# Self-attention of a three-stage block: scores a step ahead, token rows, V with zero blocks, and the softmax's sum before the next maximum

## The chip, the cores and the metric

The program runs on one core of a Trainium2 chip. Its time is the device time of one execution in microseconds (us). Its engines run side by side and meet at semaphores: TensorE (PE, matmul; PEld is its weight load), VectorE (DVE), ScalarE (ACT), GpSimd (POOL), and SyncE (SP), which here only issues DMAs. Each takes its own instructions in order: what stands behind a waiting instruction waits too.

## The reference, cut to what matters

```
x = x + cross_attention(layernorm(x), ctx)      # stage 1
x = x + self_attention(layernorm(x))            # stage 2, the one that is changed
x = x + gated_ffn(layernorm(x))                 # stage 3

# stage 2, x of shape (32, 64, 256), 16 heads of 16:
qkv = x @ W_w.T + W_b
attn = q k^T / 16;  attn[future] = -inf;  attn += rpb[position difference]
o = softmax(attn) @ v                            # one 64x64 matrix per batch element and head
y = x + o @ proj_w.T + proj_b;  out = layernorm(y) * ln_g + ln_b
```

Its 2048 rows (32 batch elements of 64 tokens) are 16 tiles of 128: two batch elements a tile.

## The kernel before, in words

Stage 2 is `self_attention` (lines 838 to 1351); stages 1 and 3 stand before and behind it, each closed by a barrier of all engines, and are not touched.

**Preparation.** DVE normalises the tiles (`normal`). Work of four tiles (a group r of 0 to 3) is cut into units, listed in `SETUP` (before the loop) and `BESIDE` (units inside step s): TN transposes rows, QK makes a 128x512 block of queries or keys (PE; ACT evicts it twice, as float16 QK_HI and as float32; POOL makes QK_LO, their difference), VV makes V rows (DVE evicts them), WT transposes part of stage 3's gate weight, and XT transposes the result for stage 3. For every group SP then issues 36 DMAs that stack the three float16 products (hi·hi, hi·lo, lo·hi) in 96 partitions: 12 into SQS (queries, L940), 24 into KZ (keys, L948), whose other half-heads are zeros that POOL has written (L1153, L1165). PE waits for the 36 at the first tile of a group. SP's first wait is for QK_LO (L935).

**The loop** runs s from 0 to 18, a pipeline over tiles:
- PE: scores of tile s (L1012, 32 matmuls of 64 columns), `PT`x`V` of tile s-2 (L1025, 32 matmuls with 16 columns of V), projection of s-3 (L1037, 4 matmuls), the step's units, and last the eight transposes of tile s-1's probabilities (L1050), which wait for POOL's scaling of s-1.
- DVE: add the bias to the scores (L1291, into T), row maximum (L1295), both of tile s; then residual and statistics of s-3 (L1299, L1301), units, and last sum and reciprocal of s-1 (L1312, L1314).
- POOL: subtract the maximum, tile s (L1175); scale by the reciprocal, tile s-1 (L1180).
- ACT: copy PT and OT of tile s-2 (L1112, L1115), lay V of s-1 into VS with zeros around it (L1122), exponential of tile s (L1125), and units behind it.

Scores stand with (head parity, query) in the partitions, so bias and V have to be repeated or laid out for each of the two batch elements w. In steps 13 to 16 DVE also has the end of the layer norm: `scale_rows` (aggregates and twelve small dependent operations) and `add_rows` (three operations a tile).

The order within each engine is the order of the statements. The steps are unrolled by Python, without a planner.

Of the kernel before, what the change touches and what calls it, by code (L numbers as in the profile page):

```python
# [43 lines left out]
C_ID, C_HM, C_DM, C_IQ, C_HQ, C_B1 = 0, 128, 130, 138, 202, 204  # L44
C_ALL = C_B1 + 1


def constants():
    c = np.zeros((P, C_ALL), np.float32)
    p = np.arange(P)  # L50
    c[:, C_ID:C_ID + P] = np.eye(P)
    for a in range(2):
        c[:, C_HM + a] = (p % 32) // DH == a
        c[:, C_HQ + a] = np.where(p < ROW_M, c[:, C_HM + a], 1.0)
    for j in range(PAIRS):
# [755 lines left out]
def turned(xr, c):  # L811
# [8 lines left out]
]  # L820
BESIDE = {
# [7 lines left out]
NARROW = 2  # L829
NORMS = [(0, 10), (10, 14), (14, 16)]  # L830
# [7 lines left out]
def self_attention(nc, sb, ctx, dram):  # L838
# [4 lines left out]
    def psum(name, shape):  # L843
# [16 lines left out]
    V = alloc("V2", [P, TILES, D], F32)  # L860
    VS = alloc("VS", [P, 2, 2, D], F32)
# [6 lines left out]
    OT = alloc("OT2", [P, 2, 4, P], F32)  # L868
# [3 lines left out]
    WN = PT[:, :, :, :].rearrange("p u j r -> p (u j r)")[:, 0:WCOLS]  # L872
# [9 lines left out]
             "vs bias_ok xb init zeroed s_ps t_a t_max t_sub t_exp t_sum t_norm p_ps pt pv ot y_ps y_sb y_stat "  # L882
# [3 lines left out]
    N_SMALL = 5  # L886
    PARTS = 36

# [17 lines left out]
    def emptied(eng, x):  # L906

        done = {"TN": "xlo", "QK": "qk_32", "VV": "v_sb", "WT": "wg_lo", "XT": "xt_sb"}[x[0]]
        eng.wait_ge(sm[done], number[x] + 1)

    def qk_rows(i):
        return i
# [12 lines left out]
    def _(sp):  # L925
        sp.dma_start(WRAW[:, :, :], dram["w_t"].rearrange("(k p) n -> p k n", p=P)).then_inc(sm["in_w2"], 16)
        sp.dma_start(BQK[:, :], dram["bqk"]).then_inc(sm["in_small"], 16)
        for tile, name in ((BV, "bv2"), (LG, "ln_g"), (LB, "ln_b")):
            sp.dma_start(tile[:, :], dram[name].rearrange("(a d) -> a d", a=1).broadcast_to([P, D])).then_inc(sm["in_small"], 16)
        sp.dma_start(BIAS[:, :, :], dram["bias"]).then_inc(sm["in_small"], 16)  # L930
        sp.dma_start(WN.rearrange("p (f d) -> p f d", f=FT), dram["w_gate"].rearrange("(f p) d -> p f d", p=P)).then_inc(sm["in_wg"], 16)
        sp.dma_start(WP[:, :, :], dram["wp"]).then_inc(sm["in_wp"], 16)
        for r in range(TILES // 4):
            u = r % 2
            sp.wait_ge(sm["qk_lo"], 4 * r + 2)  # L935
            if r >= 2:
                sp.wait_ge(sm["s_ps"], 4 * (r - 1))
            for c in range(4):
                for q, part in enumerate((QK_HI, QK_HI, QK_LO)):
                    sp.dma_start(SQS[32 * q:32 * q + 32, u, c::4, :], part[32 * c:32 * c + 32, u, 0:2, :]).then_inc(stacked[r], 16)  # L940
            sp.wait_ge(sm["qk_lo"], 4 * r + 4)
            if r < 2:
                sp.wait_ge(sm["zeroed"], r + 1)
            for c in range(4):
                for q, part in enumerate((QK_HI, QK_LO, QK_HI)):
                    for a in range(2):
                        lo = 32 * q + DH * a
                        sp.dma_start(KZ[lo:lo + DH, u, c::4, a, :], part[32 * c + DH * a:32 * c + DH * a + DH, u, 2:4, :])\  # L948
                            .then_inc(stacked[r], 16)
        for r in range(TILES // 4):  # L950
            sp.wait_ge(stacked[r], 16 * PARTS)

    @block.tensor
    def _(pe):

        def setup(x):
# [11 lines left out]
            elif kind == "QK":  # L968
                m = qk_rows(i)
# [5 lines left out]
                for e, (w, h, k) in enumerate([(w, h, k) for w, h in ((WHI, 0), (WHI, 1), (WLO, 0)) for k in range(KT)]):  # L975
                    last = pe.matmul(bank, w[:, k, m * P:(m + 1) * P], XR[:, r, h, k, :], start=(e == 0), stop=(e == 5))
                last.then_inc(sm["qk_ps"], 1)
            elif kind == "VV":
                pe.wait_ge(sm["xlo"], 2 * r + 2)
                for s in range(2):  # L980
                    lo = (2 * i + s) * P
                    for e, (h, w, k) in enumerate([(h, w, k) for k in range(KT) for h, w in ((0, WHI), (0, WLO), (1, WHI))]):
                        last = pe.matmul(bank[:, s * D:(s + 1) * D], XR[:, r, h, k, lo:lo + P], w[:, k, 2 * D:3 * D],
                                         start=(e == 0), stop=(e == 5), skip_group_check=True)
# [14 lines left out]

        for x in SETUP:  # L1000
            setup(x)
        for s in range(STEPS):
            if live(s):
                r, lo = s // 4, s % 4 * P
                if s % 4 == 0:
                    pe.wait_ge(stacked[r], 16 * PARTS)
                need(pe, sm["t_a"], s)
                for j in range(PAIRS):
                    for w in range(2):
                        cols = slice(lo + w * SQ, lo + (w + 1) * SQ)  # L1010
                        for a in range(2):
                            last = pe.matmul(S_PS[SQ * a:SQ * (a + 1), (2 * j + w) * SQ:(2 * j + w + 1) * SQ], SQS[0:96, r % 2, j, cols],  # L1012
                                             KZ[0:96, r % 2, j, a, cols], start=True, stop=True, skip_group_check=True)
                last.then_inc(sm["s_ps"], 1)
            if live(s - 2):
                t = s - 2
                if t == 0:
                    pe.wait_ge(sm["init"], 3)
                pe.wait_ge(sm["pt"], t + 1)
                pe.wait_ge(sm["vs"], 2 * t + 2)  # L1020
                need(pe, sm["ot"], t)
                for w in range(2):
                    for h in range(H):
                        row = 32 * (h % 4)
                        last = pe.matmul(O_PS[row:row + DH, (h // 4) * P + w * SQ:(h // 4) * P + (w + 1) * SQ],  # L1025
                                         VS[:, t % 2, w, h * DH:(h + 1) * DH],
                                         PT[:, t % 2, h // 2, (h % 2) * SQ:(h % 2 + 1) * SQ],
                                         start=True, stop=True, skip_group_check=True)
                last.then_inc(sm["pv"], 1)
            if live(s - 3):  # L1030
                t = s - 3
                if t == 0:
                    pe.wait_ge(sm["in_wp"], 16)
                pe.wait_ge(sm["ot"], t + 1)
                need(pe, sm["y_sb"], t)
                for g in range(4):
                    last = pe.matmul(Y_PS[:, 0:D], OT[:, t % 2, g, :], WP[:, g, :], start=(g == 0), stop=(g == 3))  # L1037
                last.then_inc(sm["y_ps"], 1)
            for x in BESIDE.get(s, []):
                setup(x)  # L1040
            if live(s - 1):
# [7 lines left out]
                for j in range(PAIRS):  # L1049
                    last = pe.transpose(T_PS[:, j * P:(j + 1) * P], T[:, t % 3, j, :, :].rearrange("p w k -> p (w k)"),  # L1050
# [6 lines left out]
    def _(act):  # L1057

        def setup(x):
# [3 lines left out]
            if kind == "TN":  # L1063
# [35 lines left out]

        act.wait_ge(sm["ln2"], LN_ROOT)  # L1100
        nc.scalar.activation(SD[:, :], VE[:, :], ACT.Sqrt).then_inc(sm["root2"], 1)
        for x in SETUP:
            setup(x)
        act.wait_ge(sm["init"], 3)
        for s in range(STEPS):
            if live(s - 2):
                t = s - 2
                if t == 0:
                    act.wait_ge(sm["wg_lo"], 4)
# [5 lines left out]
                nc.scalar.activation(OT[:, t % 2, :, :], O_PS[:, :].rearrange("p (g r) -> p g r", g=4), ACT.Copy).then_inc(sm["ot"], 1)  # L1115
            if live(s - 1):
                t = s - 1
                need(act, sm["pv"], t - 1)
                act.wait_ge(sm["v_sb"], t // 2 + 1)
                for w in range(2):  # L1120
                    rows = slice(64 * w, 64 * w + 64)
                    nc.scalar.activation(VS[rows, t % 2, w, :], V[rows, t, :], ACT.Copy).then_inc(sm["vs"], 1)  # L1122
# [8 lines left out]
            for x in BESIDE.get(s, []):  # L1131
                setup(x)
# [9 lines left out]
    def _(pool):  # L1142

        def setup(x):

            kind, r, i = x
            if kind == "QK":
                n, m = number[x] + 1, qk_rows(i)
                pool.wait_ge(sm["qk_32"], n)
                pool.tensor_tensor(QK_LO[:, r % 2, m, :], QK32[:, (n - 1) % 3, :], QK_HI[:, r % 2, m, :], ALU.subtract)\  # L1150
                    .then_inc(sm["qk_lo"], 1)

        pool.memset(KZ[:, 0].rearrange("p j a c -> p (j a c)").bitcast(F32), 0.0).then_inc(sm["zeroed"], 1)  # L1153
# [579 lines left out]
```

## Time and profile before

| | us |
|---|---|
| median of 3 runs (1729.69, 1731.11, 2875.7) | 1731.11 |
| the profiled execution: device time | 1730.49 |
| its span, first to last instruction | 1728.7 |
| stage 2 in it: 1246.69 to 1541.46 | 294.8 |
| of that, before the first scores (1299.07) | 52.4 |

Busy over the whole span: PE 84%, DVE 63%, ACT 52%, POOL 49%. In stage 2 alone the sums are PE 155.4, DVE 151.3, POOL 104.9 and ACT 96.1 us of 294.8, so no engine is full there; what counts is what each waits for. The 2875.7 is one run far off the other two.

### The profile page before, as it was taken

To read this page: it belongs to the slowest core of one execution; us is meant where nothing else is said; L and a number is where in the kernel's file an instruction comes from. 1 tells how busy PE (TensorE), PEld (TensorE's weight loads), DVE (VectorE), ACT (ScalarE), POOL (GpSimd) and SP (SyncE) were. 2 spreads that over 40 slices of the span, in tenths; PEclk is the share of its full clock that TensorE was granted. 3 is DMA by queue.
4 is the path that set the end of the run, shared out by engine and by line. 5 is a ranking of instruction groups with operands and counts; after the bars stand their busy time and mean duration, and the time that the engine had idled before them with its cause. 6 is when DMAs were issued, how large, how long until landed. Compare 5 with 4: busy or idle time off the path is not lost. (4 is left out here: it accounts for less than half of the span.)

```text
span 1728.7 us, 55875 instructions
## 1 busy us (share of the span) xinstructions
PE 1450.7 (84%) x24601; PEld 1018.8 (59%) x24601; DVE 1081.6 (63%) x1736; ACT 900.0 (52%) x1196; POOL 839.4 (49%) x555
## 2 busy tenths in 40 slices
PE   3789999999999999999999999999655655457607
PEld 2357777677776777766777767777424444333206
DVE  7656666666666666666666666666353444586985
ACT  1446555566556665566665556656433322143752
POOL 5567655666655666556665566653053443202000
PEclk9899999999999999999999999999876876678958
DMA  5544544334444344443454534543122110010001
GB/s 171 134 118 103 126 115 136 105 98 123 120 112 133 98 117 123 114 134 98 108 129 108 143 99 101 128 115 69 31 70 52 26 38 1 1 37 0 1 0 49
DMA packets 90688, 154.94 MB, mean 90 GB/s; under 512 B 17280, under 2 KB 55816, under 8 KB 90448
## 3 DMA queue, kind: packets, MB, share of 16 engines
q1 hardware_dynamic: 89088, 150.40, 33.4%
q8 instruction: 195, 3.19, 0.8%
q10 hardware_dynamic: 1360, 0.98, 0.2%
q14 instruction: 45, 0.37, 0.1%
HBM read 60.95 MB, written 2.20 MB: 37 GB/s over the span
## 5 line engine op out<-in xcount | busy, mean ns | idle before, releaser
L639 DVE TENSOR_REDUCE MXP<-W_PS 128x1 f32<-128x512 f32 x768 | 499.2, 688 | 283.4 <-PE W_PS L451 283.4
L535 ACT ACTIVATE PR<-S_PS 128x1024 f32<-128x1024 f32 (+1 forms) x416 | 424.9, 1023 | 258.6 <-PE S_PS L399 250.8
L345 POOL TENSOR_TENSOR K_HI<-K,MCOL 128x512 f16<-128x512 f32 (+1 forms) x224 | 219.0, 978 | 425.3 <-ACT K L543 424.0
L347 POOL TENSOR_TENSOR K_LO<-K,K_HI 128x512 f16<-128x512 f32 (+1 forms) x224 | 291.8, 1302 | 17.6
L451 PE MATMUL W_PS<-STK,QS 105*128 105x512 f16 (+1 forms) x1024 | 269.8, 335 | 9.0 <-POOL STK L372 4.8
L399 PE MATMUL S_PS<-QS,STK 105*128 105x128 f16 (+1 forms) x3328 | 256.0, 220 | 1.0 <-DVE QS L653 1.0
L414 PEld LDWEIGHTS O_PS<-PR,V 128*17 128x17 f32 x13312 | 191.0, 98 | 79.2 <-issue 59.1
L414 PE MATMUL O_PS<-PR,V 128*17 128x64 f32 x13312 | 231.3, 220 | 7.6 <-ACT PR L535 7.5
L434 PE MATMUL W_PS<-WV_HI,CTX_HI 128*128 128x256 f16 (+1 forms) x832 | 228.3, 274 | 1.6 <-DVE WV_LO L612 1.4
L434 PE MATMUL W_PS<-WV_HI,CTX_LO 128*128 128x256 f16 (+1 forms) x832 | 227.7, 274 | 0.0
L434 PE MATMUL W_PS<-WV_LO,CTX_HI 128*128 128x256 f16 (+1 forms) x832 | 227.6, 274 | 0.0
L399 PEld LDWEIGHTS S_PS<-QS,STK 105*128 105x128 f16 (+1 forms) x3328 | 201.3, 99 | 44.4 <-DVE QS L653 1.1
L351 POOL TENSOR_TENSOR CTX_LO<-CTX,CTX_HI 128x3202 f16<-128x3202 f32 x32 | 194.2, 6069 | 10.4 <-DVE CTX_HI L617 10.2
L558 ACT ACTIVATE V<-W_PS 128x512 f32<-128x512 f32 (+1 forms) x224 | 127.0, 567 | 131.5 <-PE W_PS L434 125.8
L543 ACT ACTIVATE K<-W_PS,BK 128x512 f32<-128x512 f32 (+1 forms) x256 | 145.3, 594 | 96.1 <-PE W_PS L425 89.3
L425 PE MATMUL W_PS<-CTX_HI,WK_HI 128*128 128x512 f16 (+1 forms) x512 | 128.0, 334 | 1.7 <-ACT K L543 1.4
L425 PE MATMUL W_PS<-CTX_LO,WK_HI 128*128 128x512 f16 (+1 forms) x512 | 127.2, 332 | 0.0
L425 PE MATMUL W_PS<-CTX_HI,WK_LO 128*128 128x512 f16 (+1 forms) x512 | 126.2, 333 | 0.0
L451 PEld LDWEIGHTS W_PS<-STK,QS 105*128 105x128 f16 x1024 | 84.8, 98 | 46.9 <-DVE MXP L639 9.2
L434 PEld LDWEIGHTS W_PS<-WV_HI,CTX_HI 128*128 128x128 f16 (+1 forms) x832 | 82.6, 99 | 29.5 <-DVE WV_LO L612 1.5
L434 PEld LDWEIGHTS W_PS<-WV_LO,CTX_HI 128*128 128x128 f16 (+1 forms) x832 | 83.0, 100 | 18.7 <-issue 0.8
L1050 PE MATMUL T_PS<-CST,T 128*128 128x128 f32 x128 | 28.9, 400 | 73.4 <-POOL T L1180 73.4
(243 smaller groups left out, 1713.3 us busy)
## 6 DMA issues: line engine op xcount, KB each, us to landing
CTX<-in_ctx_t SPq DMA_DIRECT2D x64, 800.5 KB, 5.9
STK<-K_HI SPq DMA_DIRECT2D x256, 128.0 KB, 2.6
STK<-K_HI SPq DMA_DIRECT2D x256, 72.1 KB, 2.1
STK<-K_LO SPq DMA_DIRECT2D x128, 128.0 KB, 2.6
STK<-K_LO SPq DMA_DIRECT2D x128, 72.1 KB, 2.1
QSTK<-STK SPq DMA_DIRECT2D x12, 192.0 KB
SQS<-QK_HI SPq DMA_DIRECT2D x32, 64.0 KB, 2.0
KZ<-QK_HI SPq DMA_DIRECT2D x64, 32.0 KB, 2.0
```

Of the source, the lines that this page charges most:

```text
L345: pool.tensor_tensor(K_HI[:, m, lo:hi], k32, zero, ALU.add).then_inc(k_hi, 1)
L347: pool.tensor_tensor(K_LO[:, m, lo:hi], k32, K_HI[:, m, lo:hi], ALU.subtract).then_inc(k_lo, 1)
L351: pool.tensor_tensor(CTX_LO[:, u, :, :], CTX[:, :, :], CTX_HI[:, u, :, :], ALU.subtract).then_inc(ctx_lo, 1)
L399: last = pe.matmul(S_PS[par][0:m, j * 2 * SQ:(j + 1) * 2 * SQ], STK[u][0:KROWS, j, i * P:i * P + m], QS[0:KROWS, u, j, :, :], start=True, ...
L414: last = pe.matmul(O_PS[r:r + VW, (h // 4) * SQ:(h // 4 + 1) * SQ], V[u][0:m, i, h, :], PR[0:m, par, h * SQ:(h + 1) * SQ], start=(i == 0 a ...
L425: last = pe.matmul(bank[:, s * LAST:s * LAST + hi - lo], a[0][:, c_, m * P:(m + 1) * P], a[1][:, u, c_, lo:hi], start=(e == 0), stop=(e == ...
L434: last = pe.matmul(bank[0:hi - lo, s * D:(s + 1) * D], a[0][:, w, k, lo:hi], a[1][:, k, :], start=(e == 0), stop=(e == 5), skip_group_chec ...
L451: last = pe.matmul(bank[:, s * LAST:s * LAST + hi - lo], QS[0:KROWS, w, j, :, :], STK[w][0:KROWS, j, lo:hi], start=True, stop=True, skip_g ...
L535: nc.scalar.activation(PR[0:m, par, :], S_PS[par][0:m, :], ACT.Exp).then_inc(p_sb, 1)
L543: nc.scalar.activation(K32[:, i % 4, cols], bank[:, cols], ACT.Identity, bias=BK[:, m:m + 1], scale=1 / W_SCALE).then_inc(k_32, 1)
L558: nc.scalar.activation(V[w][0:m, t0:t1, :, 0:DH], bank[0:m, 0:(t1 - t0) * D].rearrange("p (t h d) -> p t h d", t=t1 - t0, h=H), ACT.Copy, ...
L639: dve.tensor_reduce(MXP[:, j, at:at + 1], bank[:, :], AX.X, ALU.max).then_inc(mx_done, 1)
```

## The change

1. **Scores a step ahead.** PE issues the scores of tile s+1 at the head of step s (and of tile 0 before the loop), before the transposes of s-1 and not behind them.
2. **Sum before maximum.** DVE: add(s), sum and reciprocal (s-1), maximum(s), then the rest. POOL: scaling of s-1 before the subtraction of s. Sum and scaling of a tile so stand ahead of the next tile's maximum.
3. **Token rows.** Scores stand with (batch element, query) in the partitions and (head, key) in the columns: 16 matmuls of 128 columns. BIAS is full size (128x1024, loaded twice into 64 partitions) and added without a repeat. Transposed, the partitions are (head parity, key).
4. **V with zero blocks.** V is written by DVE as 32-column blocks, a head pair each, with zeros in the opposite corners, and two groups are kept. VV is 48 matmuls with 64 columns of weights, evicted in two halves of 64 partitions. PT x V is 16 matmuls, OT half as wide (256), the projection 2 matmuls. VS and ACT's copies into it go. V's bias goes through the projection once, into BP, which POOL adds to the residual rows (`RESIDUAL`: steps 0, 1, 4, 7).
5. **Zeros.** ACT writes a tile of zeros and the first half of KZ (5 copies of 1024 columns); DMAs from that tile zero V's first half (1 MB, in the preparation) and, behind the first group's 36 DMAs, KZ's second half (1.57 MB) and V's (1.05 MB). The keys of group 1 wait for both. POOL's two memsets and DVE's three go.
6. **Stacking in three rounds.** SP starts with the DMAs that need QK_HI only (8 of the queries, 16 of the keys) and issues those of QK_LO (4 and 8) last. POOL makes the QK_LO of the first four units before anything else.
7. **Later work.** The gate weight is loaded behind group 1's DMAs; its scales are made in step 3, its rounding in 5 and 6, its transposes in 8 and 9. The units of `BESIDE` are spread anew; ACT does them before the step's exponential. ACT's exponential table is loaded before the loop.

The order of DVE in steps 4 and 5, before (T is the scores with bias, MX the maximum, SM the sum and reciprocal, XN the residual rows):

```order
L1291 TENSOR_TENSOR T<-S_PS,BIAS 128x1024
L1295 TENSOR_REDUCE MX<-T 128x16
L1299 TENSOR_TENSOR XN<-Y_PS,XN 128x256
L1301 BN_STATS STAT<-XN 128x6
L1200 TENSOR_TENSOR XR<-R_PS,XR 128x2x256 x2
L1312 TENSOR_REDUCE SM<-T 128x16
L1314 RECIPROCAL SM<-SM 128x16
L1291 TENSOR_TENSOR T<-S_PS,BIAS 128x1024
```

and in the changed kernel:

```order
L1336 TENSOR_TENSOR T<-S_PS,BIAS 128x1024
L1342 TENSOR_REDUCE SM<-T 128x16
L1344 RECIPROCAL SM<-SM 128x16
L1348 TENSOR_REDUCE MX<-T 128x16
L1354 TENSOR_TENSOR XN<-Y_PS,XN 128x256
L1356 BN_STATS STAT<-XN 128x6
L1336 TENSOR_TENSOR T<-S_PS,BIAS 128x1024
```

The sum moved from the end of the step to its second place, and the TN unit to step 3.

PE around the transposes of step 4, before (T_PS are transposed probabilities, S_PS scores, O_PS is PT x V, Y_PS the projection):

```order
L1050 MATMUL T_PS<-CST,T 128x128 x8
L1012 MATMUL S_PS<-KZ,SQS 64x64 x32
L1025 MATMUL O_PS<-PT,VS 16x64 x32
L1037 MATMUL Y_PS<-WP,OT 128x256 x4
L966 MATMUL R_PS<-CST,XN 128x128 x8
```

and after:

```order
L1088 MATMUL T_PS<-CST,T 128x128 x8
L1040 MATMUL S_PS<-KZ,SQS 64x128 x16
L1067 MATMUL O_PS<-PT,V 32x64 x16
L1047 MATMUL Y_PS<-WP,OT 128x256 x2
L1005 MATMUL R_PS<-XR,WHI 128x512 x4
```

The kinds stand in the same order, but the scores behind those transposes are now of the tile that DVE takes a step later, so nothing waits for them there; and there is half as much of each.

SP between group 0 and group 2, in the changed kernel (V and KZ from T are the zeros):

```order
L951 DMA SQS<-QK_LO 32x2x512 x4
L957 DMA KZ<-QK_LO 16x2x512 x8
L939 DMA KZ<-T 96x4x1024
L939 DMA V<-T 128x2x1024
L951 DMA SQS<-QK_HI 32x2x512 x8
L957 DMA KZ<-QK_HI 16x2x512 x16
L951 DMA SQS<-QK_LO 32x2x512 x4
L957 DMA KZ<-QK_LO 16x2x512 x8
L978 DMA WRAW<-in_w_gate 128x6x256
```

Before, group 1's 36 DMAs stood right behind group 0's.

The core of the diff:

```
@@ SP
-            sp.wait_ge(sm["qk_lo"], 4 * r + 2)
...
+            if r == 1:
+                zero(KZ[:, 1]..., 4, zeroed[1])
+                zero(V[:, 1]..., 2, zeroed[1])
+            sp.wait_ge(sm["qk_hi"], 4 * r + 2)
+            if r >= 2:
+                sp.wait_ge(sm["s_ps"], 4 * (r - 1))
+            queries(0, QK_HI)
+            queries(1, QK_HI)
+            sp.wait_ge(sm["qk_hi"], 4 * r + 4)
...
+            elif r == 1:
+                sp.wait_ge(zeroed[1], 32)
+            keys(0, QK_HI)
+            keys(2, QK_HI)
+            sp.wait_ge(sm["qk_lo"], 4 * r + 4)
+            queries(2, QK_LO)
+            keys(1, QK_LO)
@@ PE
+        scores(0)
         for s in range(STEPS):
-            if live(s):
...
+            if live(s + 1):
+                scores(s + 1)
@@ DVE, VV unit
-                dve.scalar_tensor_tensor(V[:, t:t + 2, :], bank..., 1 / W_SCALE, BV..., ALU.mult, ALU.add)
+                for a in range(2):
+                    rows = slice(SQ * a, SQ * (a + 1))
+                    dve.tensor_scalar(V[rows, r % 2, 4 * i:4 * i + 4, :, DH * a:DH * (a + 1)], bank[rows, :]..., 1 / W_SCALE, None, ALU.mult)
@@ DVE, step 3
+            if s == 3:
+                dve.wait_ge(sm["in_wg"], 16)
+                dve.tensor_reduce(WS[:, :], blk, AX.X, ALU.max, apply_absolute_value=True).then_inc(sm["wg_max"], 1)
```

## Rows read from the trace of the kernel before

**Rows 1.** Windows: start:end, length, busy (count) by engine, PE clock, DMA, GB/s.
```profile
1246.69:1299.07 52.38, 23.88 (x125) 13.90 (x125) 29.84 (x61) 16.80 (x27) 25.83 (x14) 0.73 0.28 84
1299.07:1346.60 47.53, 28.04 (x376) 20.21 (x376) 17.44 (x20) 17.60 (x26) 17.85 (x11) 0.72 0.22 54
1346.60:1451.25 104.65, 66.97 (x1064) 52.11 (x1064) 44.70 (x58) 36.22 (x56) 47.94 (x26) 0.79 0.09 22
1451.25:1505.55 54.30, 24.04 (x376) 19.56 (x376) 28.60 (x68) 11.51 (x19) 11.39 (x6) 0.67 0.00 1
1505.55:1541.46 35.91, 12.51 (x120) 9.49 (x120) 30.73 (x117) 14.01 (x26) 1.90 (x1) 0.72 0.00 1
```
**Rows 2.** Timeline, step 10: start, length, engine, line, names, idle before.
```profile
1417.77 1.23 DVE L1291 TENSOR_TENSOR T<-S_PS,BIAS 128x1024 f32<-128x1024 f32 x1 [4.76 <-PE S_PS L1012]
...
1417.84 1.52 PE L1025 MATMUL O_PS<-PT,VS 128*16 128x64 f32 x64
1419.03 1.22 DVE L1295 TENSOR_REDUCE MX<-T 128x16 f32<-128x1024 f32 x1
...
1419.29 1.99 PE L1037 MATMUL Y_PS<-WP,OT 128*128 128x256 f32 x8
...
1420.33 1.90 POOL L1175 TENSOR_TENSOR T<-T,MX 128x1024 f32<-128x1024 f32 x1 [3.03 <-DVE MX L1295]
...
1422.12 1.20 DVE L1312 TENSOR_REDUCE SM<-T 128x16 f32<-128x1024 f32 x1
1422.26 1.06 ACT L1125 ACTIVATE T<-T 128x1024 f32<-128x1024 f32 x1 [1.49 <-POOL T L1175]
...
1423.69 1.90 POOL L1180 TENSOR_TENSOR T<-T,SM 128x1024 f32<-128x1024 f32 x1 [1.46 <-DVE SM L1314]
...
1425.64 1.97 PE L1050 MATMUL T_PS<-CST,T 128*128 128x128 f32 x8 [4.36 <-POOL T L1180]
...
1428.65 1.22 DVE L1291 TENSOR_TENSOR T<-S_PS,BIAS 128x1024 f32<-128x1024 f32 x1 [5.04 <-PE S_PS L1012]
```
**Rows 3.** Timeline of the preparation, same columns; SPq is a DMA issue.
```profile
1246.69 3.51 POOL L1153 MEMSET KZ<- 96x4096 f32 x1 [54.22 <-POOLq L1675]
...
1247.93 2.30 DVE L786 TENSOR_SCALAR VE<-MV 128x16 f32<-128x16 f32 x1
...
1262.69 0.69 ACT L1077 ACTIVATE QK_HI<-T_PS,BQK 128x512 f16<-128x512 f32 x1 [0.51 <-PE T_PS L976]
...
1273.30 1.23 SPq L940 DMA_DIRECT2D SQS<-QK_HI  x2
...
1296.39 1.26 SPq L948 DMA_DIRECT2D KZ<-QK_HI  x2
```
**Rows 4.** DMA view, 1246 to 1400: issues, KB each, median us to landing.
```profile
KZ<-QK_HI SPq DMA_DIRECT2D x58, 32.0 KB, 2.0
...
WRAW<-in_w_t SPq DMA_DIRECT2D x1, 768.0 KB, 4.4
```
**Rows 5.** Groups by form in 1240 to 1545: busy, mean ns, idle before.
```profile
L1150 POOL TENSOR_TENSOR QK_LO<-QK,QK_HI 128x512 f16<-128x512 f32 x16 | 19.9, 1256 | 9.9 <-ACT QK L1080 9.8
...
L1185 POOL TENSOR_TENSOR X<-X,LB 128x1024 f32<-128x1024 f32 x4 | 9.4, 2353 | 0.0
...
L1205 DVE SCALAR_TENSOR_TENSOR V<-R_PS,BV 128x512 f32<-128x512 f32 x6 | 4.0, 686 | 4.7 <-PE R_PS L983 4.7
...
L1240 DVE TENSOR_SCALAR PT<-PT 128x1536 f32<-128x1536 f32 x1 | 1.8, 1786 | 0.0
```
**Rows 6.** Timeline of step 13 on DVE, columns as in group 2.
```profile
1456.03 0.77 DVE L1253 BATCH_NORM_AGGREGATE MV<-STAT 128x2 f32<-128x6 f32 x10
1456.84 0.17 DVE L1255 TENSOR_SCALAR VE<-MV 128x10 f32<-128x10 f32 x1
...
1459.30 0.48 DVE L1273 SCALAR_TENSOR_TENSOR XN<-XN,MV,LG 128x256 f32<-128x256 f32 x1
...
1463.42 1.20 DVE L1312 TENSOR_REDUCE SM<-T 128x16 f32<-128x1024 f32 x1
```

More of the change, by code:

```diff
@@ L885, in self_attention @@
     stacked = [sem(nc, ctx, f"stacked{r}") for r in range(TILES // 4)]
-    N_SMALL = 5
+    zeroed = [sem(nc, ctx, f"zeroed_{s}") for s in ("first", "second")]
     PARTS = 36
+    N_SMALL = 7
     units = SETUP + [x for s in range(STEPS) for x in BESIDE.get(s, [])] + ENDING
@@ L906, in emptied @@
     def emptied(eng, x):
[L908 to L912, printed above, removed]
+        done, each = {"TN": ("xlo", 1), "QK": ("qk_32", 1), "VV": ("v_sb", 2), "WT": ("wg_lo", 1), "XT": ("xt_sb", 1)}[x[0]]
+        eng.wait_ge(sm[done], each * (number[x] + 1))
     wgroups = [(k, range(o, o + 3)) for o in range(0, FT, 3) for k in range(KT)]
@@ L931, in _, with zero @@
-        sp.dma_start(WN.rearrange("p (f d) -> p f d", f=FT), dram["w_gate"].rearrange("(f p) d -> p f d", p=P)).then_inc(sm["in_wg"], 16)
-        sp.dma_start(WP[:, :, :], dram["wp"]).then_inc(sm["in_wp"], 16)
+        sp.dma_start(WP[:, :, :], dram["wp"].rearrange("(g p) n -> p g n", p=P)).then_inc(sm["in_wp"], 16)
+        sp.wait_ge(sm["zero"], 1)
+        def zero(dst, n, done):
+            rows = dst.shape[0]
+            sp.dma_start(dst.rearrange("p (n z) -> p n z", n=n), ZERO[0:rows].unsqueeze(1).broadcast_to([rows, n, PAIRS * 2 * SQ]))\
+                .then_inc(done, 16)
@@ L933, in _ @@
+        zero(V[:, 0].rearrange("p t j c -> p (t j c)"), 2, zeroed[0])
         for r in range(TILES // 4):
             u = r % 2
-            sp.wait_ge(sm["qk_lo"], 4 * r + 2)
[L936 to L939, printed above, removed]
-                    sp.dma_start(SQS[32 * q:32 * q + 32, u, c::4, :], part[32 * c:32 * c + 32, u, 0:2, :]).then_inc(stacked[r], 16)
-            sp.wait_ge(sm["qk_lo"], 4 * r + 4)
@@ L942, in _, with queries @@
[L942 to L945, printed above, removed]
+            if r == 1:
+                zero(KZ[:, 1].rearrange("p j a c -> p (j a c)").bitcast(F32), 4, zeroed[1])
+                zero(V[:, 1].rearrange("p t j c -> p (t j c)"), 2, zeroed[1])
+            def queries(q, part):
+                for c in range(4):
+                    sp.dma_start(SQS[32 * q:32 * q + 32, u, c::4, :], part[32 * c:32 * c + 32, u, 0:2, :]).then_inc(stacked[r], 16)
@@ L946, in _, with keys @@
+            def keys(q, part):
+                for c in range(4):
                     for a in range(2):
@@ L998, in setup, with scores @@
                 last.then_inc(sm["xt_ps"], 1)
+        def scores(t):
+            r, lo = t // 4, t % 4 * P
+            if t % 4 == 0:
+                pe.wait_ge(stacked[r], 16 * PARTS)
+            need(pe, sm["t_a"], t)
+            for j in range(PAIRS):
+                for w in range(2):
+                    cols = slice(lo + w * SQ, lo + (w + 1) * SQ)
+                    last = pe.matmul(S_PS[SQ * w:SQ * (w + 1), j * P:(j + 1) * P], SQS[0:96, r % 2, j, cols],
+                                     KZ[0:96, r % 2, j, :, cols], start=True, stop=True, skip_group_check=True)
+            last.then_inc(sm["s_ps"], 1)
@@ L1000, in _, with project @@
+        def project(outs):
+            for g in range(KT):
+                last = pe.matmul(Y_PS[:, 0:D], outs[:, g, :], WP[:, g, :], start=(g == 0), stop=(g == KT - 1))
+            return last
         for x in SETUP:
             setup(x)
+        pe.wait_ge(sm["in_wp"], 16)
+        pe.wait_ge(sm["bp_row"], 1)
+        project(OT[:, 0]).then_inc(sm["bp_ps"], 1)
+        scores(0)
         for s in range(STEPS):
-            if live(s):
[L1004 to L1007, printed above, removed]
+            if live(s + 1):
+                scores(s + 1)
+            if live(s - 2):
+                t = s - 2
+                pe.wait_ge(sm["pt"], t + 1)
+                pe.wait_ge(sm["v_sb"], 2 * (t // 2 + 1))
+                need(pe, sm["ot"], t)
@@ L1008, in _ @@
                 for j in range(PAIRS):
                     for w in range(2):
[L1010 to L1028, printed above, removed]
+                        row, col = 32 * (j % 4), j // 4 * P + w * SQ
@@ L1029, in _ @@
+                        last = pe.matmul(O_PS[row:row + 32, col:col + SQ], V[:, t // 4 % 2, 2 * (t % 4) + w, j, :],
+                                         PT[:, t % 2, j, w * SQ:(w + 1) * SQ], start=True, stop=True, skip_group_check=True)
                 last.then_inc(sm["pv"], 1)
@@ L1114, in _ @@
                 need(act, sm["y_ps"], t - 1)
[L1115 to L1122, printed above, removed]
+                if t == 0:
+                    act.wait_ge(sm["bp_ps"], 1)
+                nc.scalar.activation(OT[:, t % 2, :, :], O_PS[:, 0:D].rearrange("p (g r) -> p g r", g=KT), ACT.Copy).then_inc(sm["ot"], 1)
+            for x in BESIDE.get(s, []):
+                if x[0] != "XT":
+                    setup(x)
             if live(s):
@@ L1220, in _ @@
         normal(range(0, 4))
-        normal(range(4, 8))
         setup(SETUP[0])
```

222 lines of the change are left out of this document (124 added, 98 removed), and 8 rows, old and new, of tables (BESIDE, SETUP).

## The prediction

> **What bounds the kernel now.** I read the windows first, cut at five events of stage 2: its start, the first scores (1299.07), DVE's bias addition of tile 4 (1346.60) and of tile 13 (1451.25), the residual addition of tile 13 in step 16 (1505.55), and the end [rows 1]. The reader should see 294.8 us in which DVE, the busiest engine beside PE, works half the time. Nine steps take 104.65 us, 11.6 each, in which DVE works 5.0 a step and PE 7.4. So the loop is bound by waits in a ring.
>
> The timeline of one step shows the ring [rows 2]. From one bias addition (1417.77) to the next (1428.65) are 10.9 us. DVE adds and takes the maximum, then waits for PE's projection (which waited for PT x V, and that for ACT's copy of the transposes), does the residual, and only then the sum of the tile before (1422.12). POOL scales from 1423.69, PE transposes from 1425.64, and the next scores stand behind the transposes. Every engine is passed once, in series. In the preparation, the first scores wait for 36 DMA issues, from 1273.30 to 1297.65 [rows 3].
>
> **The change, part by part.** I go through the same five stretches.
>
> *A, preparation (52.4 before).* POOL's memset of 3.51 goes from the start; beside it DVE's VE took 2.30, which in step 13 takes 0.17 [rows 3, 6]. So up to 2.1 us come back; ACT's new zero tile and its table load leave about 1.2 (bounds 0 and 2.1). The stacking no longer waits for QK_LO but for the second QK_HI, which ends at 1262.69 + 0.69 = 1263.4, so now at 1262.2. The same 36 issues and the landing took 1299.07 - 1273.30 = 25.8, so the first scores come at 1288.0: **-11.1**. What this is hidden behind: PE must have done its units by then. VV's 48 narrow matmuls have no row; if they take twice the old unit's time, PE still ends some us ahead of 1288, so I take nothing (bounds 0 and +5). The five zeroing copies are 1 us each on ACT, in which it waits for PE.
>
> *B, first four steps (47.5 before).* Here a new wait appears. Group 1's keys wait for 2.62 MB of zeros. 768 KB landed in 4.4 us and 32 KB in 2.0 [rows 4], so 0.79 MB cost 2.4 more than nearly nothing and 2.62 MB cost 8 + 2 = 10 us. SP issues the zeros at 1288.0 - 1.4 + 1.0 = 1287.6 (8 issues run beside them), they land at 1297.6; 28 more issues at 24.35/36 = 0.68 less the hiccup, so 0.64, end at 1315.5, landed 1317. The scores of tile 4 are wanted some 22 us after the first (steps of 5.5 to 8.5), at about 1310: a stall of 7. Behind it on PE stand PT x V and the projection (1 us each now), DVE's residual of tile 0, the TN unit (3.3 through PE, ACT and DVE) and, new in step 3, the weight's scales. Their load is issued last by SP and lands 4.4 later, at 1320.5, ahead of DVE, which reaches it at 1324.2; the maximum over 1536 columns is 1.5 x 1.22 and with its two small followers 2.6. Bias addition of tile 4: 1326.8, 38.8 after the first scores: **-8.7**. Bounds of the zeros: no stall beyond the steps' own, -16; the price of small DMAs is a rival below.
>
> *C, steps 4 to 12 (104.65 before).* The new ring is: exponential(s-1) done, sum and reciprocal 1.57 (from the sum's start to the scaling's), scaling 1.90, subtraction 1.90, exponential 1.06 [rows 2], about 0.1 for the last hand-over: 6.5. Off it are the transposes (1.97), scores (16 matmuls for 32), PT x V (1.52, half the matmuls), the projection (1.99, now half) and ACT's copies: together at most 6.5 on PE, and they have a whole step. The maximum runs beside the scaling. DVE needs 1.23 + 1.57 + 1.22 and 0.9 for residual and statistics, 5.0: it fits. A clean step is 6.5 (step 12). With units:
> - 4 and 5: POOL has 3.8, a residual addition (2.35, as the LB addition of the same shape) or 1.5 x 1.90 = 2.85 of weight work, and two QK_LO at 1.16 to 1.26 [rows 5]: 8.5 and 9.0; with hand-overs 8.8 and 9.2. ACT's two QK pairs stand before the exponential and would give nearly the same.
> - 6: DVE has 5.0, two V evictions and two rounding passes of 1.79 [rows 5]: 10.5.
> - 7, 10, 11: V evictions. The old one is 0.69 for 128x512; the new are two of 64 partitions with the same columns, so I take 2 x 0.65 (bounds: 0.69 if partitions halved the time, 3 if the short output runs hurt). 6.5 + 1.3 = 7.9, 8.0, 8.0.
> - 8, 9: two weight units, 7.0 each; the LB addition fits POOL's gap of 2.7.
> Sum 8.8 + 9.2 + 10.5 + 7.9 + 14.0 + 16.0 + 6.5 = 72.9: **-31.8**.
>
> *D, steps 13 to 15 and the sum of 16 (54.3 before).* DVE is the bound: 5.0 + aggregates and chain 3.3 (1456.03 to 1459.30) + three tiles' rows 4.1 (to 1463.42) [rows 6] = 12.4; then 9.1 and 9.1; then 1.6: 32.2. Added to it is 3 us for a collision. The new order puts POOL's subtraction (until 3.9 us into the step) beside `add_rows`, which begins at 5.0 - 1.2 after the sum began; VE's 2.30 against 0.17 shows that DVE can stand still for a POOL instruction. 35.2: **-19.1**. The Trainium skill (SBUF — State Buffer, on the shared port pair) says that a DVE instruction with two SBUF inputs and a GpSimd one that reads SBUF exclude each other for a whole instruction, "the loser fully blocks", and that a plain reduction never contends. By that rule the collision is up to 1.9 in each of three steps, 5.7, and never touches the loop's sums and maxima; this trace shows the block only with a memset.
>
> *E, the end (35.9 before).* The sum of tile 15 (1.5) has gone to D, and the last projection is a us shorter: **-2.5**.
>
> Sum: 11.1 + 8.7 + 31.8 + 19.1 + 2.5 = 73.2. Stages 1 and 3 stay as they are. 1730.5 (profiled, 0.6 below the median shown) - 73.2 = **1657.3**.
>
> Two edits cost nothing by cover. ACT's VS copies and their replacement by zeros lie off the ring (ACT 36 of 104.65). POOL's residual additions in steps 0 and 1 run in the stall before tile 4; without that stall they would cost 2 us in step 1.
>
> **The rivals.**
> 1. *The forecast*, chance 0.50: about 1657.
> 2. *PE and ACT stay in the ring.* The granted clock in the loop is 0.67 to 0.79 [rows 1], so much work runs at the lower of the two levels. At 1.2 GHz a QK pair holds ACT's exponential back by 2.5 us in each of steps 4 and 5, and if each clean step takes 8 and not 6.5 (one more hand-over through ACT's queue, where the exponential stands behind two copies that wait for PE), C loses 5 + 7 x 1.5 = 15.5: 1673. For it: ACT's order. Against: PE has more than half a step to spare. Chance 0.22. The Trainium skill (TensorE: Matmul & The Clock Gate, on oscillation) says that idle gaps return PE to the low rate. By that rule the shorter loop, whose gaps are shorter, would be granted more and not less.
> 3. *No stall at tile 4*: the zeros land early or the steps before it are slow anyway, and V's evictions cost 0.7. B is better by 6 and C by 2: 1649. Chance 0.15.
> 4. *The ring is not cut.* If some engine's order still ties the transposes to the next sum, C and D gain only what DVE's and PE's shorter work gives (2 us a step in twelve): 11.1 + 8.7 + 24 + 2.5, so 1684. For it: T has three buffers and T_PS one. Against: in the order of statements the scores of tile s+1 need only the addition of s. Chance 0.09.
> 5. *Slower than before: the zeros crawl.* 32 KB take 2.0 us to land [rows 4]. If the SBUF-to-SBUF zeros went at that pace, 16 KB/us, V's first MB would take 64 us and hold V's eviction, and so the first scores, to about 1316; the other 2.62 MB take 160, and tile 4 waits for them. Against 10 us in B this is +150, and A +28: the time is 1835. It decides from a zeroing time of about 83 us, when the 73 are used up. Against: those rows are latency, the WRAW row moves 24 times the bytes in 4.4. Chance 0.04.
>
> **How the numbers follow.** The time is that of the forecast. The range takes in rival 3 on one side and rival 2 on the other, with A's +5, V's upper bound (6 us) and the spread of D's collision: 1641 to 1682. Outside are rivals 4 and 5 and tails. Faster by over 2% means below 1696, about what a measurement can tell: rivals 1, 2, 3 and nearly all of 4, 0.92; the same 0.04; slower 0.04.
>
> **What would show it.** After: first scores about 41 us into stage 2; a wait of PE for KZ at tile 4 of some 7 us; sum to sum 6.5 us in step 12, with POOL's scaling and subtraction back to back and ACT's exponential right behind; steps 13 to 15 with DVE full; transposes that nobody on DVE waits for. Wrong would be: POOL idle between scaling and subtraction, scores released later than the addition of the tile before, or DVE waiting for PE's scores in clean steps.

## The result, and the profile after

The changed kernel takes 1662.87 us (median of 4 runs, 1662.41 to 1664.57) against 1732.12 in the same session. That median has the one far run of 2875.7 among its four; the ratio, 0.961 with a 95% interval of 0.959 to 0.963, is taken from the other three, whose median is 1731.11. The forecast was 1657: the span of the profiled execution became 66.3 us shorter, 7 short of the 73.2 worked out. Stage 2 went from 294.8 to 227.5.

The windows of the changed kernel, cut at the same five events, answer to [rows 1] (start:end, length, busy (count) of PE, PEld, DVE, ACT, POOL, then PE clock, DMA share, GB/s):

```profile
1246.50:1289.37 42.87, 22.17 (x260) 13.57 (x260) 14.94 (x49) 21.59 (x30) 11.53 (x10) 0.74 0.43 110
1289.37:1334.00 44.63, 19.28 (x212) 12.83 (x212) 22.91 (x30) 14.84 (x21) 22.22 (x13) 0.70 0.52 130
1334.00:1401.86 67.86, 48.86 (x760) 35.72 (x760) 49.70 (x70) 26.02 (x37) 55.63 (x29) 0.87 0.15 35
1401.86:1439.63 37.77, 19.13 (x208) 14.49 (x208) 30.94 (x70) 9.41 (x12) 13.75 (x9) 0.67 0.00 1
1439.63:1473.98 34.35, 13.74 (x80) 10.38 (x80) 28.99 (x114) 14.02 (x26) 1.65 (x1) 0.60 0.00 1
```

| stretch | before | after | gain | forecast |
|---|---|---|---|---|
| A, to the first scores | 52.38 | 42.87 | 9.5 | 11.1 |
| B, to the addition of tile 4 | 47.53 | 44.63 | 2.9 | 8.7 |
| C, to the addition of tile 13 | 104.65 | 67.86 | 36.8 | 31.8 |
| D, to the residual of tile 13 | 54.30 | 37.77 | 16.5 | 19.1 |
| E, the end | 35.91 | 34.35 | 1.6 | 2.5 |

Stage 3, which is untouched, is 1.2 longer in this execution, stage 1 0.2 shorter. The largest gap is B. Step 12 on all engines (timeline of the changed kernel: start, length, engine, line, names, idle before) is the new ring, to be read against [rows 2]:

```profile
1398.56 1.21 DVE L1342 TENSOR_REDUCE SM<-T 128x16 f32<-128x1024 f32 x1
1398.70 0.64 PE L1040 MATMUL S_PS<-KZ,SQS 96*64 96x128 f16 x16 [1.74 <-DVE T L1336]
...
1399.98 1.16 DVE L1348 TENSOR_REDUCE MX<-T 128x16 f32<-128x1024 f32 x1
...
1400.14 1.90 POOL L1212 TENSOR_TENSOR T<-T,SM 128x1024 f32<-128x1024 f32 x1 [2.09 <-DVE SM L1344]
1401.06 0.42 DVE L1354 TENSOR_TENSOR XN<-Y_PS,XN 128x256 f32<-128x256 f32 x1
...
1402.00 1.90 POOL L1216 TENSOR_TENSOR T<-T,MX 128x1024 f32<-128x1024 f32 x1
...
1403.93 1.06 ACT L1167 ACTIVATE T<-T 128x1024 f32<-128x1024 f32 x1 [3.51 <-POOL T L1216]
1405.02 1.22 DVE L1342 TENSOR_REDUCE SM<-T 128x16 f32<-128x1024 f32 x1 [1.96 <-ACT T L1167]
```

Sum to sum is 6.46 (forecast 6.5), POOL's two operations stand back to back, the exponential right behind, and the residual (L1354) waits for nobody. Where B's time went, DVE's timeline from the preparation to the first bias addition shows (same columns):

```profile
1267.41 2.84 DVE L1259 TENSOR_SCALAR V<-R_PS 64x512 f32<-64x512 f32 x4
1301.32 2.85 DVE L1259 TENSOR_SCALAR V<-T_PS 64x512 f32<-64x512 f32 x4 [31.07 <-DMA V<-T]
1304.20 0.69 DVE L1286 TENSOR_SCALAR BIAS<-BIAS 128x1024 f32<-128x1024 f32 x1
1304.92 0.42 DVE L1288 TENSOR_TENSOR BP<-Y_PS,BP 128x256 f32<-128x256 f32 x1
1305.26 1.22 DVE L1336 TENSOR_TENSOR T<-S_PS,BIAS 128x1024 f32<-128x1024 f32 x1
```

DVE stands 31 us in front of the V eviction of group 1, whose target has to be zero first. SP issues that zeroing behind the 36 DMAs of group 0 (SP's timeline, the second V<-T):

```profile
1252.87 0.70 SPq L939 DMA_DIRECT2D V<-T  x1
1262.54 6.03 SPq L951 DMA_DIRECT2D SQS<-QK_HI  x8
...
1287.96 0.62 SPq L939 DMA_DIRECT2D KZ<-T  x1
1288.62 0.66 SPq L939 DMA_DIRECT2D V<-T  x1
1289.32 11.67 SPq L951 DMA_DIRECT2D SQS<-QK_HI  x8
```

It lands 12.7 us later, at 1301.3. The first scores began at 1289.37 and ended at 1290.4, but the first bias addition, behind that eviction on DVE, starts at 1305.26, later than before the change (1300.24).

### The profile page after: what moved, and what is told of

Its sections match the earlier page's. It is cut to its first block and busy times, and to the rows that moved or that the text cites. A ratio compares the mean times of both kernels' runs of the same rounds, so it can differ in the third digit from the quotient of the medians.

```text
span 1662.4 us, 54781 instructions
## 1 busy us (share of the span) xinstructions
PE 1421.2 (85%) x24061; PEld 991.0 (60%) x24061; DVE 1077.9 (65%) x1743; ACT 889.0 (53%) x1170; POOL 839.3 (50%) x557
## 5 line engine op out<-in xcount | busy, mean ns | idle before, releaser
L433 PEld LDWEIGHTS W_PS<-WV_HI,CTX_LO 128*128 128x128 f16 (+1 forms) x832 | 82.3, 99 | 9.3
## 6 DMA issues: line engine op xcount, KB each, us to landing
V<-T SPq DMA_DIRECT2D x2, 1024.0 KB, 10.4
```

The costliest lines, as they stand in the source:

```text
L433: last = pe.matmul(bank[0:hi - lo, s * D:(s + 1) * D], a[0][:, w, k, lo:hi], a[1][:, k, :], start=(e == 0), stop=(e == 5), skip_group_chec ...
```

## The experiments

All times are medians of 4 runs, ratios against the kernel before on the same chip. Kernels of one group ran together; the kernel before took 1731.91, 1731.35 and 1732.43 in the three groups. The interval of a ratio is about 0.0015 wide to each side, 2.6 us, so a difference of 5 us between kernels of different groups is only just clear of it. Letters A to E are the stretches of the table above, and a clean step is one whose units add nothing to its ring.

**First group: which part of the order brings it.**

*Sum late.*

```
 DVE, step s
-  [sum, reciprocal of s-1]
   [maximum of s, residual of s-3, units, add_rows]
+  [sum, reciprocal of s-1]
 POOL
-  [scaling of s-1]
   [subtraction of s]
+  [scaling of s-1]
```

> The changed kernel, but sum and reciprocal of tile s-1 stand at the end of DVE's step again, and POOL subtracts before it scales. Theory 1 (the place of the sum cuts the ring): the scaled tile comes late, and PE's transposes hold the scores, PT x V and the projection behind them, for which DVE's residual waits ahead of the sum. Ring at the high clock: sum and reciprocal 1.46, scaling 1.90, transposes 1.09, scores 0.64, PT x V 0.69, projection 1.13, residual and statistics 0.85, hand-overs 0.6: 8.4 a clean step, at the low clock 11. Nine steps give back 18 to 40 us, steps 13 to 16 about 12, the first steps 4: 1697 to 1715. Theory 2 (scores a step ahead and the shorter work bring it, the sum's place is indifferent): DVE has 5.1 us of work a step, so clean steps stay at 6.5 or below and the time is 1655 to 1668.

1720.16, ratio 0.994 (0.992 to 0.995). Theory 1's mechanism, at 5 us above its range. Its step 12 (timeline):

```profile
1427.84 1.90 POOL L1216 TENSOR_TENSOR T<-T,SM 128x1024 f32<-128x1024 f32 x1 [5.50 <-DVE SM L1374]
...
1429.80 1.97 PE L1088 MATMUL T_PS<-CST,T 128*128 128x128 f32 x8 [5.03 <-POOL T L1216]
1431.70 1.06 PE L1040 MATMUL S_PS<-KZ,SQS 96*64 96x128 f16 x16
...
1432.88 1.11 PE L1067 MATMUL O_PS<-PT,V 128*32 128x64 f32 x32
1433.92 1.94 PE L1047 MATMUL Y_PS<-WP,OT 128*128 128x256 f32 x4
...
1435.89 0.42 DVE L1347 TENSOR_TENSOR XN<-Y_PS,XN 128x256 f32<-128x256 f32 x1 [5.62 <-PE Y_PS L1047]
...
1436.70 1.20 DVE L1372 TENSOR_REDUCE SM<-T 128x16 f32<-128x1024 f32 x1
```

The late scaling holds the transposes, these hold the scores, PT x V and the projection, and DVE's residual waits 5.62 for the projection with the sum behind it. In the nine steps of C, DVE waits 47.1 for the projection, and they take 102.51 (67.86 in the changed kernel). PE works at 1.2 GHz in much of it: transposes 1.97 and not 1.09, projection 1.94 and not 1.13, granted clock of the stretch 0.73 against 0.87.

*Scores late.*

```
 PE
-  scores(0)
   for s:
-      scores(s + 1)
+      scores(s)
```

> The changed kernel, but PE computes the scores of tile s at the head of step s and not in step s-1. Theory 1 (two rings, the sum's is the one that matters): a new ring add 1.23, sum and reciprocal 1.46, scaling 1.90, transposes 1.09, scores 0.64 and hand-overs 0.6 is 7.0 us at the high clock, 8.4 at the low, against 6.5: the time is 1668 to 1682, and DVE waits for the scores in every step. Theory 2 (scores ahead is the larger half): clean steps of 9 and more, 1690 to 1700. Theory 3 (indifferent): 1663, no wait of DVE for scores.

1663.69, ratio 0.961 (0.959 to 0.962): the changed kernel's own. Theory 3's time, but not its reason: DVE does wait for the scores, 13.6 us in C. DVE's waits there (us in total, times, longest), in this kernel and then in the changed one:

```profile
DVE T L1335 <- PE S_PS L1040: 13.6, 8, 4.6
DVE XN L1353 <- PE Y_PS L1047: 2.2, 2, 1.5
```

```profile
DVE SM L1342 <- ACT T L1167: 8.8, 3, 4.4
DVE XN L1354 <- PE Y_PS L1047: 5.1, 5, 1.5
```

The wait takes the place of others. The additions come later (tile 13 at 1404.76 and not 1401.86), the sums hardly (tile 12 at 1405.90 and not 1405.02, tile 15 at 1437.74 and not 1437.82). From sum to sum the nine steps take 70.56 against 69.94, 0.07 a step. The ring of 7.0 through the scores, which I expected to bind, is not the limit: steps 8 and 10 take 6.46 from sum to sum, as in the changed kernel.

*Both late* is the two edits together. What is left of the change is all but the order: the layout, the zeros, the stacking in three rounds and the later weight work. No run separates these, and below "the rest" means all of them.

> The changed kernel with the old order on PE, DVE and POOL: only the layout (token rows, V's zero blocks, zeroing by DMA) is left of the change. Theory 1: the ring of the kernel before with shorter scores, PT x V and projection, 8.9 at the high clock and 10.3 at the low, against 10.9 before; order is worth about 44 us: 1700 to 1715. Theory 2 (the shorter work on PE and ACT brings most): under 1680.

1724.22, ratio 0.996 (0.994 to 0.997), above theory 1's range: DVE waits 67.5 us for the scores. The rest without the order brings 8 us. In the profiled execution A is 10.0 shorter than before and B 4.7 longer.

*Order alone* is the opposite: the kernel before with the scores, the sum and the scaling moved, nothing else.

> The kernel before, with nothing but the new order: scores a step ahead on PE, sum ahead of the maximum on DVE, scaling ahead of the subtraction on POOL. Theory 1: the preparation stays at 52 us; in the loop the ring of 6.5 is gone as the limit and PE's old work, 7.4 a step on average, is the limit: nine steps take 72 to 80 and not 105, steps 13 to 16 gain about 12: 1685 to 1695. Theory 2 (order without the layout brings little, since ACT's copies of PT and OT and the stacked scores stay in the ring): above 1710.

1668.47, ratio 0.964 (0.963 to 0.966), better than theory 1. I had taken PE's old work as the limit of a step. It isn't: its steps 10 to 12 are 6.47, 6.48, 6.47 us, as short as with the new layout. The 7.4 a step was PE's work at a granted clock of 0.79. In the nine steps of C here (1337.15 to 1403.74) the granted clock is 1.00 and PE works 49.9 us, 5.5 a step. Addition, sum and residual of step 12 (DVE's timeline):

```profile
1397.27 1.21 DVE L1296 TENSOR_TENSOR T<-S_PS,BIAS 128x1024 f32<-128x1024 f32 x1
1398.95 1.22 DVE L1302 TENSOR_REDUCE SM<-T 128x16 f32<-128x1024 f32 x1 [0.48 <-ACT T L1130]
...
1402.93 0.42 DVE L1312 TENSOR_TENSOR XN<-Y_PS,XN 128x256 f32<-128x256 f32 x1 [1.40 <-PE Y_PS L1042]
```

So, with this order, the layout's shorter matmuls are worth nothing in a clean step.

**Second group: V's zeros, and what the sum must stand ahead of.**

*V's zeros early.*

```
 SP, preparation
   zero(V[:, 0], zeroed[0])
+  zero(V[:, 1], v1_zero)
 SP, ahead of group 1
   zero(KZ[:, 1], zeroed[1])
-  zero(V[:, 1], zeroed[1])
 DVE
+  addition of tile 2 waits for zeroed[1]   (it overwrites the tile of zeros)
```

> The changed kernel, but the zeros of V's second group are issued right behind those of the first, in the preparation, not behind the 36 transfers of group 0; the keys' zeros of group 1 stay where they are. Theory 1 (DVE's V eviction, held until 1301.3 by these zeros, held the first bias addition): the 31.1 us wait is gone and the first addition starts 0.6 us behind the first scores, at about 1290.6 against 1305.3; the steps 0 to 3 then run into the keys of group 1, whose zeros (1.5 MB less 1 MB before them) land 3 us sooner: addition of tile 4 at about 1326 to 1328 and not 1334.0, so 1654 to 1657. Theory 2 (the first addition was not what set tile 4; the keys of group 1 land when they land): the first addition moves by 14, tile 4 by nothing: 1661 to 1664.

1657.27, ratio 0.958 (0.956 to 0.959): theory 1, at 0.3 above its range. The first addition starts at 1290.34 (expected 1290.6), that of tile 4 at 1327.86. Now the stall that the prediction had named at tile 4, 7 us, is there (PE's timeline):

```profile
1304.08 0.64 PE L1040 MATMUL S_PS<-KZ,SQS 96*64 96x128 f16 x16
1318.68 1.06 PE L1040 MATMUL S_PS<-KZ,SQS 96*64 96x128 f16 x16 [7.93 <-DMA KZ<-QK_LO]
```

In the changed kernel it was hidden behind the 15 us that DVE lost before: its scores of tile 4 start at 1324.73 with no wait for the keys.

*Zeros by POOL.*

```
 POOL, start of the preparation
+  wait for the first four normalised tiles
+  memset(V[:, 1]); memset(KZ[:, 1])     (p_zero)
 SP, ahead of group 1
-  zero(KZ[:, 1], zeroed[1]); zero(V[:, 1], zeroed[1])
```

> The changed kernel, but the second-group zeros of V and of the keys are two POOL memsets at the start of the preparation, where POOL idles until 1261, and SP has no zeros between group 0 and group 1. Theory 1: as v_zero_early for the first addition (about 1291), and the keys of group 1 land at about 1311, the weight's load at 1316: addition of tile 4 at about 1320 against 1334.0, so 1647 to 1651. Theory 2 (POOL's memsets, 3.5 us for the keys and about 1.8 for V, block DVE beside them as in the kernel before, VE 2.30 against 0.18): the preparation is later by up to 5 us: 1652 to 1656. Theory 3 (tile 4 is not set by these zeros): 1661 to 1664.

1650.15, ratio 0.953 (0.952 to 0.955); theory 1. The two memsets, in POOL's idle time, and the first addition (timelines of POOL and DVE):

```profile
1252.99 1.81 POOL L1194 MEMSET V<- 128x2048 f32 x1 [59.51 <-DVE XN L1272]
1254.73 3.52 POOL L1195 MEMSET KZ<- 96x4096 f32 x1
```

```profile
1290.62 1.22 DVE L1336 TENSOR_TENSOR T<-S_PS,BIAS 128x1024 f32<-128x1024 f32 x1 [10.58 <-PE S_PS L1037]
```

The addition of tile 4 is at 1321.94 (expected 1320), PE waits 2.33 for the keys there. Theory 2's cost isn't there: the first scores start at 1289.44, in the changed kernel at 1289.37. This does not test whether a memset holds VE up, since the edit lets POOL start only when VE is done (1248.95). Beside the memsets WLO takes 1.76 as in the changed kernel, the next normalisations 4.24 in place of 3.96.

*Subtraction first* keeps DVE's order and swaps only POOL's two operations back.

> The changed kernel, but POOL subtracts tile s's maximum before it scales tile s-1; DVE's sum stays ahead of the maximum. Theory 1 (the sum's place on DVE is what cut the ring, POOL's order is worth little): the ring is sum and reciprocal 1.46, maximum 1.16, subtraction 1.90, exponential 1.06, hand-overs 0.3: 5.9 a clean step against 6.5, while PE's transposes come 3 us later but have the slack: 1657 to 1664. Theory 2 (the scaling must stand first, since the transposes hold PT x V, projection and DVE's residual): DVE waits for the projection again, 8 us a clean step: 1675 to 1685.

1677.54, ratio 0.969 (0.967 to 0.970): theory 2's time. DVE's wait for the projection, from 1334 to 1416 (us in total, times, longest), is less than the 8 a clean step it had named:

```profile
DVE XN L1354 <- PE Y_PS L1047: 15.5, 7, 4.4
```

In steps 9 to 11, one of 6.60 stands between two of 10.4. My slack for the transposes was wrong: 1.9 us later on POOL cost 15 us.

*Maximum first.*

```
 DVE, step s
   [addition of s]
+  [maximum of s]
   [sum, reciprocal of s-1]
-  [maximum of s]
 POOL: subtraction of s, then scaling of s-1
```

> The changed kernel, but DVE takes the maximum of tile s before the sum of tile s-1 (both still ahead of the residual), and POOL subtracts before it scales. Theory 1 (what matters is that the sum stands ahead of the residual, which waits for PE; against the maximum its place is free): no ring holds sum, maximum, subtraction and exponential in one step any more; DVE's work, 5.1 a step, or half of the ring over two steps (sum, scaling, transposes, scores, PT x V, projection, residual, addition, maximum: 11 at the high clock, 13.5 at the low) is the limit, 5.5 to 6.8 a clean step: 1653 to 1665. Theory 2 (the sum must stand ahead of the maximum, as the words of the change have it): as the kernel with the sum late, clean steps near 10: 1700 to 1720.

1666.63, ratio 0.963 (0.962 to 0.964). Theory 2 is out; the time is 1.6 above the upper end of theory 1. Addition of tile 4 to that of 13 takes 68.5 us, against 67.9. What the sum has to stand ahead of is the residual, which waits for PE, not the maximum, which the title names. (POOL's order was swapped along with DVE's here; the maximum first with POOL's scaling first was not run.) Why swapping POOL's operations costs little here and 15 us in the kernel before it: the scaling, which releases the transposes, starts 2.7 us after the step's addition in the changed kernel, 4.4 here (1397.10 to 1401.52 in step 12) and 5.7 with the subtraction first (1397.97 to 1403.63 in step 11). That the limit lies between 4.4 and 5.7 is read from these three, not tried.

**Third group.** *Sum alone* is the kernel before with the sum and the scaling moved, the scores left in their place.

> The kernel before, with nothing but the sum ahead of the maximum on DVE and the scaling ahead of the subtraction on POOL; the scores stay where they were. Theory 1 (the sum's place is the whole of it, as the runs with the sum late and the scores late say): as the kernel with the whole order, 1665 to 1672. Theory 2 (in the old layout, with PE's longer scores, PT x V and projection, the scores' place counts): the ring addition 1.23, sum and reciprocal 1.46, scaling 1.90, transposes 1.09 to 1.97, 32 score matmuls 1.3 to 2.0, hand-overs 0.6 is 7.6 to 9.2 a clean step against 6.47: 1678 to 1690.

1674.04, ratio 0.967 (0.966 to 0.969), between the two. DVE waits 36 us for scores in stage 2, and clean steps of 6.43 alternate with steps of 8 to 9.6. In the old layout the scores' place is worth the 5.6 us from here to 1668.47.

*Zeros by POOL and maximum first.*

> The kernel with the POOL memsets, and the order of the kernel with the maximum first. Theory 1 (the two edits lie in different stretches and add up, and the second was worth nothing up to the addition of tile 15): 1650 to 1654. Theory 2 (with tile 4 earlier and POOL subtracting first in steps 0 to 3, where DVE waits 4.9 and 2.9 us for the exponential, the maximum first shortens them by up to 3): 1645 to 1648.

1652.14, ratio 0.954 (0.952 to 0.955): theory 1. The edits don't help each other: 1652.14 and 1650.15 are within the noise, and no kernel here is faster than these two.

The account from 1732, each step a kernel that ran:

| | us | step |
|---|---|---|
| before | 1732 | |
| + sum and scaling ahead | 1674.0 | -58 |
| + scores a step ahead | 1668.5 | -5.6 |
| + the rest: the changed kernel | 1662.9 | -5.6 |
| + second zeros by POOL | 1650.2 | -12.7 |

The shares depend on the path. Sum and scaling come first either way, and are worth 58 in the old layout and 60.5 in the new (1724.22 to 1663.69). Behind them, the rest brings 10.4 while the scores stand late (1674.04 to 1663.69), and then the scores 0.8. The two overlap by 4.8 us. The small step of the rest hides larger ones. Set against the kernel with the order alone, the changed kernel is 9.7 shorter in A, 2.9 in D, and longer in the others: 8.0 in B, 1.3 in C, 0.9 in E. Most of what the preparation gained was lost again in B, where the late zeros are; with POOL's zeros B takes 32.5 and not 44.6.

## Why the prediction was right, and where not

**C, the ring: right in kind, 5 us too dear, of which 2 only moved.** The clean step (6.46 for 6.5), POOL's pair back to back and the free transposes came as named. The forecast was 72.9 for nine steps; between the additions they took 67.86, but from sum to sum, which is the ring, 69.94. The difference of 2.1 lies in where the window is cut: the addition of tile 13 comes 3.16 ahead of its step's sum, that of tile 4 only 1.08, and DVE pays for it in D with a wait of 2.0 for the exponential. Of the other 3 us, 1.7 is step 6 (8.83 for 10.5). Its two rounding passes cost 0.96 each, where I had taken 1.79 from [rows 5]. In that row four QK_LO of POOL ran beside the pass (from 1269.59, for 6.10); in step 6 POOL was idle, from 1358.63 to 1361.03. So the 1.79 was likely a price beside POOL, and I took it for the price alone; no run separates the two. Another 1.2 is steps 10 and 11, where part of the units fitted into DVE's spare 1.5 us.

Rival 2, PE and ACT in the ring, did not come: the granted clock rose from 0.79 [rows 1] to 0.87. With the sum late it was 0.73, and with the order alone 1.00. This agrees with the rule quoted from the Trainium skill (TensorE: Matmul & The Clock Gate, on oscillation).

**But the reason was too wide.** The prediction gave the cut to the whole order. The runs show that the scores a step ahead bring 0.8 us in the new layout (1663.69 to 1662.87, inside the spread) and 5.6 in the old, and that PE's shorter work brings a clean step nothing. The rival "the ring is not cut" priced DVE's and PE's shorter work at 2 us a step; with both orders late, the nine steps take 102.2 (1344.23 to 1446.42) of 104.65, 0.3 a step.

**A, the preparation: 1.6 short.** VE takes 0.18 where it took 2.30 [rows 3], and the first queries are issued at 1262.54 (forecast 1262.2). The rest is issue time: 36 issues take from 1262.54 to 1287.92, 25.4 in place of 24.35.

**B, the first steps: the step that failed.** I had written "PE must have done its units by then" and costed the new eviction at nothing. PE was done; DVE was not. The eviction of group 1's V waits for zeros that SP issues behind 36 DMAs, and it stands ahead of the first addition. The prediction treated these zeros as a wait of the keys alone. The kernel with V's zeros early shows both: 15 us at the first addition, and behind it the predicted stall, 7.93 for 7. There B takes 38.69 us, for 38.8 forecast: without that wait B comes out as worked out. Rival 5 had the very mechanism, a zeroing that holds V's eviction, but let it work only with the zeros at 16 KB/us; 1 MB that landed in 12.7 us, issued late, was enough.

**D, the last tiles: 2.6 short.** Forecast 32.2 and 3 for a collision. The collision is there, in DVE's timeline beside POOL's in step 15:

```profile
1432.19 0.48 DVE L1318 SCALAR_TENSOR_TENSOR XN<-XN,MV,LG 128x256 f32<-128x256 f32 x1
1432.70 2.01 DVE L1321 SCALAR_TENSOR_TENSOR X<-XN,RS,X 128x256 f32<-128x256 f32 x1
1434.74 0.43 DVE L1323 BATCH_NORM_STATS2 STAT<-X 128x6 f32<-128x256 f32 x1
```

```profile
1432.34 2.08 POOL L1216 TENSOR_TENSOR T<-T,MX 128x1024 f32<-128x1024 f32 x1
```

The same instruction takes 0.48 elsewhere. It cost 1.6 in D and 0.65 in E. The Trainium skill (SBUF — State Buffer, on the shared port pair) says that such a pair excludes each other for a whole instruction while a plain reduction never contends; the trace agrees, DVE's maximum takes 1.16 beside POOL's scaling. It did not come three times, as its upper bound had it: in step 13 POOL's subtraction had ended at 1410.37, before `add_rows` began at 1413.29, and in step 14 the two met for 0.06. What the forecast left out is waits (DVE's, in this stretch): 3.2 for two projections at 1.2 GHz (2.08 each) and the 2.0 for the exponential that C had put off. With 32.2 and 1.6 that would be 39.0; the stretch took 37.77, so DVE's own work was about 1.2 less than I had added up.

```profile
DVE XN L1354 <- PE Y_PS L1047: 3.2, 2, 1.7
DVE SM L1342 <- ACT T L1167: 2.0, 1, 2.0
```

**Range and chances.** The time lies within the range, nearest to rival 1. The shortfalls of A, B, D and E (1.6, 5.8, 2.6, 0.9) add up to 10.9, and C gave 5.0 more than forecast. Without the 2 us that only moved from C to D, 9 stand against 3, so 3 us of the nearness of 1662.9 to 1657 are luck.

## What to carry to other kernels

In a software pipeline, look on each in-order engine for an instruction that waits for another engine and stands ahead of one that this other engine waits for: moving the sum ahead of the residual, with the scaling, was worth 58 of 69 us, and all else in a large rewrite 11. Any layout that needs zeros adds a wait to the first writer of the zeroed buffer too, not only to its reader; follow the queue that issues the zeroing up to its place, and use an engine that is idle then. A hidden stall is real as soon as its cover goes, so keep its price when you take the cover away. Before you take an instruction's price from a row, look at what the other engines did beside it.

## What the runs showed of the hardware

- DMA issues took longer right behind large transfers on the same queue: the 8 issues of group 1's queries took 11.67 us behind 2.6 MB of SBUF-to-SBUF zeros, 9.87 behind 1.5 MB and 5.06 without them. I had expected them to run beside the zeros at full pace.
- A POOL memset of 128x2048 took 1.81 us and one of 96x4096 3.52; the DMA that zeroes the same 1 MB of V took 12.7 from issue to landing, with the keys' 1.5 MB ahead of it.
- A POOL memset held up some DVE instructions and not others. Beside it VE took 2.30 in place of 0.18, and the first rounding pass of the weight 4.23 in place of 0.96; WLO, of two inputs, took 1.76 with or without it.
- Half as many score matmuls of twice the columns (16 of 96x128 for 32 of 96x64) took 0.64 us in place of 0.70: with the columns the same in all, 2048, halving the instructions brought 0.06. So "half as much of each", said above of the PE order, holds for the count of the score matmuls and not for their time.
